# Row maxima of batch 0 and of half of batch 1 are placed inside the second pair's front, GpSimd rotates batch 3, and inputs are loaded and projected batch by batch

## The reference

```python
q = (jnp.einsum('bsd,ed->bse', x, Wq) + bq).reshape(b, s, H, HD).transpose(0, 2, 1, 3)
k = (jnp.einsum('bsd,ed->bse', x, Wk) + bk).reshape(b, s, KVH, HD).transpose(0, 2, 1, 3)
v = (jnp.einsum('bsd,ed->bse', x, Wv) + bv).reshape(b, s, KVH, HD).transpose(0, 2, 1, 3)
q = _rms_norm(q)
k = _rms_norm(k)
cos, sin = _rope_tables(s, q.dtype)
q = _apply_rope(q, cos, sin)
k = _apply_rope(k, cos, sin)
...
attn = jnp.einsum('bhqd,bhkd->bhqk', q * scale, k)
attn = jnp.where(causal[None, None], attn, -jnp.inf)
attn = jax.nn.softmax(attn, axis=-1)
out = jnp.einsum('bhqk,bhkd->bqhd', attn, v).reshape(b, s, d)
return jnp.einsum('bsd,ed->bse', out, Wo) + bo
```

## Time and profile before

| | |
|---|---|
| median of 3 runs | 509.94 us (508.55 to 512.79) |
| the profiled execution | 507.93 us, its span 506.2 us |
| PE, PEld busy | 402.6 us (80%), 312.7 us (62%) |
| DVE, ACT, POOL busy | 343.6 us (68%), 242.7 us (48%), 107.5 us (21%) |
| first weight transpose, first projection | 9.98 us, 14.46 us |
| first stack transpose, first row maximum on TensorE | 39.24 us, 64.74 us |
| first exp_scores of layer 0 | 78.99 us |

### The profile page before, as it was taken

How to read it: one execution, slowest core, us unless ns; L and a number is a source line. 1 busy time by engine, 2 the same in 40 slices (tenths; PEclk the granted TensorE clock), 3 DMA queues, 4 the chain that set the end, 5 groups by cost and what they waited for, 6 DMA issues and landing times.

```text
span 506.2 us, 8074 instructions
## 1 busy us (share of the span) xinstructions
PE 402.6 (80%) x3090; PEld 312.7 (62%) x3090; DVE 343.6 (68%) x782; ACT 242.7 (48%) x432; POOL 107.5 (21%) x111
## 2 busy tenths in 40 slices
PE   2906578998885554599998688999987899999993
PEld 2506545676644443378766565667766689888883
DVE  0489698777677749576648888656946485666545
ACT  1558714655433863367557714446535324422230
POOL 4400005449311630042183000000101710000001
PEclk9957598999897886579999999999989999999998
DMA  6900020000000000000000006970000000000101
GB/s 203 296 5 1 1 70 5 3 4 1 2 2 0 0 2 0 0 1 0 3 0 1 1 1 87 116 149 3 2 0 1 0 2 1 0 1 0 43 1 42
DMA packets 13126, 13.33 MB, mean 26 GB/s; under 512 B 2904, under 2 KB 12448, under 8 KB 12832
## 3 DMA queue, kind: packets, MB, share of 16 engines
q1 hardware_dynamic: 12224, 12.54, 11.3%
q10 hardware_dynamic: 864, 0.27, 0.3%
HBM read 11.56 MB, written 1.05 MB: 25 GB/s over the span
## 4 chain that ended last, share of the span: by engine, by line
PE 60%; DVE 21%; ACT 11%; issue 3%; POOL 1%; DMA 1%; SPq 0%; DVEq 0%; POOLq 0%; ACTq 0%
PE PS L2146 12%; PE PS L2163 6%; ACT arena L750 5%; PE PS L1761 4%; PE PS L1845 4%; DVE mx L1263 3%; PE PS L2073 3%; PE PS L383 3%; PE PS L1886 3%; PE PS L2086 3%; PE PS L1813 3%; PE PS L1739 2%; PE PS L1855 2%; PE PS L1642 2%; DVE arena L1152 2%
## 5 line engine op out<-in xcount | busy, mean ns | idle before, releaser
L869 ACT ACTIVATE PT<-PS 128x512 f32<-128x512 f32 x96 | 53.5, 594 | 36.3 <-PE PS L1813 36.2
L2146 PE MATMUL PS<-arena_r 128*128 128x512 f32 x264 | 64.6, 393 | 2.2 <-ACT xT L750 2.2
L666 POOL TENSOR_SCALAR va<-mv 128x4 f32<-128x4 f32 x12 | 5.3, 443 | 273.3 <-DVE mv L1099 273.3
L2146 PEld LDWEIGHTS PS<-arena_r 128*128 128x128 f32 x264 | 48.0, 188 | 11.9 <-issue 2.7
L750 ACT ACTIVATE arena<-PS 96x1024 bf16<-96x1024 bf16 (+4 forms) x59 | 44.5, 810 | 22.5 <-PE PS L1739 11.3
L1739 PE MATMUL PS<-ident,arena 128*96 128x128 bf16 x416 | 30.7, 241 | 28.9 <-DVE arena L1142 27.5
L1739 PEld LDWEIGHTS PS<-ident,arena 128*96 128x96 bf16 x416 | 28.7, 141 | 32.7 <-DVE arena L1142 29.2
L1761 PE MATMUL PS<-masks,ident 128*128 128x512 bf16 x112 | 43.2, 386 | 4.7 <-DVE mx L1263 2.4
L1263 DVE TENSOR_REDUCE mx<-PS 128x4 f32<-128x1024 f32 x32 | 39.0, 1218 | 1.2 <-PE PS L1793 0.2
L2163 PEld LDWEIGHTS PS<-arena_r 128*128 128x128 f32 x264 | 34.4, 191 | 2.5 <-DVE arena_r L1564 0.9
L2163 PE MATMUL PS<-arena_r 128*128 128x256 f32 x264 | 35.1, 283 | 0.7 <-DVE arena_r L1564 0.7
(11 more groups left out here) (218 smaller groups left out, 904.7 us busy)
## 6 DMA issues: line engine op xcount, KB each, us to landing
arena<-in_L_ffn_w SPq DMA_DIRECT2D x16, 176.0 KB, 10.2
arena<-in_L_ffn_w SPq DMA_DIRECT2D x2, 1024.0 KB, 10.2
arena<-in_L_ffn_w SPq DMA_DIRECT2D x2, 704.0 KB, 7.5
arena<-in_fside_BxS2xS SPq DMA_DIRECT2D x1, 1024.0 KB, 12.7
out<-x SPq DMA_DIRECT2D x4, 256.0 KB, 2.5
x<-in_x SPq DMA_DIRECT2D x1, 768.0 KB, 8.6
arena<-in_L_attn_Wq SPq DMA_DIRECT2D x2, 256.0 KB, 4.5
arena<-in_L_attn_Wo SPq DMA_DIRECT2D x2, 256.0 KB, 6.4
```

The costliest lines, as they stand in the source:

```text
L869: nc.scalar.activation(PT[:, n % 2, 512 * j:512 * (j + 1)], bank(3 + j), ACT.Exp, scale=NEG_SCALE)\
L2146: last = mm(bank(2 * (n % 2) + gu), wp[c][:, gu, c_ * P:(c_ + 1) * P], xp[5][:, c, blk * 512:(blk + 1) * 512], start=(step == 0 and c == 0 ...
```

## The change

- **Loads.** SP issues ident, Wq, then x in three transfers (batch 0; batch 1; batches 2 and 3), each with a semaphore of its own for what waits; Wk and Wv go to the head of ScalarE's queue. The count of semaphores is kept down by dropping unused ones.
- **Projection batch by batch.** TensorE transposes batch 0, projects tiles 0 and 1, transposes batches 1 and 2, projects tiles 2 and 3, transposes batch 3 and projects the rest. ScalarE's copy of batch 3 goes behind its first squares. The waits for tables and constants stand after the projections.
- **GpSimd rotates batch 3** with seven instructions of its own; it starts when VectorE has normed the second pair (`qk_normed`), and hi_part(3) waits for `last_rotated`.
- **Maxima early.** EARLY is 6: the four groups of batch 0 and two of batch 1 stand in the front. VectorE takes two groups after the thresholds, one after each rem_part of the second pair, splits batch 0's maxima, and takes the other two between its stack copies. All six use banks 0 to 2. On TensorE batch 0's four groups stand ahead of the stack transposes of batch 2, and batch 1's two behind those of batch 2 and of batch 3.
- **ScalarE's order.** abs_sums moves from ahead of hi_part(0) to behind the stack copies of batch 0, and writes to another place; hi_part(2) goes ahead of batch 1's stack copies, hi_part(3) behind them and woT's copy.

The diff, cut:

```diff
-        def score_set(m):
-
+        EARLY = NG + 2
+
+        def score_set(L, m):
+
+            if L == 0 and m < EARLY:
+                return 0
             return 3 * (1 - m % 2) if m < LAG * NG else 0
...
             sp.dma_start(ident[:, :], t["ident"]).then_inc(w["ident"], 16)
+            sp.dma_start(wq0n[:, 0:2, :], t["L0_attn_Wq"].rearrange("(r p) d -> p r d", p=P)).then_inc(w["l0"], 16)
             sp.dma_start(x[:, 0:2, :], xv[:, 0:2, :]).then_inc(x_loaded, 16)
-            sp.dma_start(wq0n[:, 0:2, :], t["L0_attn_Wq"].rearrange("(r p) d -> p r d", p=P)).then_inc(w["l0"], 16)
-            sp.dma_start(wq0n[0:64, 2, :], t["L0_attn_Wk"]).then_inc(w["l0"], 16)
-            sp.dma_start(wq0n[64:128, 2, :], t["L0_attn_Wv"]).then_inc(w["l0"], 16)
-            sp.dma_start(x[:, 2:TT, :], xv[:, 2:TT, :]).then_inc(x_rest_loaded, 16)
+            sp.dma_start(x[:, 2:4, :], xv[:, 2:4, :]).then_inc(x1_loaded, 16)
+            sp.dma_start(x[:, 4:TT, :], xv[:, 4:TT, :]).then_inc(x_rest_loaded, 16)
...
+            def rotate(b):
+
+                pool.wait_ge(qk_normed, b // 2 + 1)
+                pool.wait_ge(w["const"], LOADS["const"])
+                pool.wait_ge(A[0]["lo"], b - 1)
+                hf = HD // 2
+                for k in range(2):
...
+                    pool.tensor_tensor(ri, qi, cos, ALU.mult)
+                    pool.tensor_tensor(si[:, :, 0:hf], qi[:, :, hf:HD], s1, ALU.mult)
+                    ins = pool.tensor_tensor(si[:, :, hf:HD], qi[:, :, 0:hf], s2, ALU.mult)
+                alone(ins)
+                ro, sq = (z[:, b % 2].rearrange("p t n -> p (t n)") for z in (qro, qsq))
+                alone(pool.tensor_tensor(ro, ro, sq, ALU.add), last_rotated)
+
+            rotate(B - 1)
...
             w = w_loaded
+            act.dma_start(wq0n[0:64, 2, :], t["L0_attn_Wk"]).then_inc(w["l0"], 16)
+            act.dma_start(wq0n[64:128, 2, :], t["L0_attn_Wv"]).then_inc(w["l0"], 16)
...
+                    evac_xT(0, 3, 4)
+
+                    hi_part(L, 0)
+                    hi_part(L, 1)
+                    mid_part(L, 0)
+                    mid_part(L, 1)
+                    squares(2)
+                    squares(3)
+                    evac_stacks(L, 0)
                     abs_sums()
...
+                    hi_part(L, 2)
+                    evac_stacks(L, 1)
+                    evac_groups(act, copy, NG0 - 1, NG0, "act")
+                    hi_part(L, 3)
+                    mid_part(L, 2)
+                    mid_part(L, 3)
+                    evac_stacks(L, 2)
+                    evac_stacks(L, 3)
                     return
...
+                    normed_queries_and_keys(2)
+                    rotate(2)
+                    thresholds()
+                    row_maxima(0, 0, 0, 0, None)
+                    row_maxima(0, 0, 1, 1, None)
+                    rem_part(0, 2)
+                    row_maxima(0, 0, 2, 2, None)
+                    rem_part(0, 3)
+                    row_maxima(0, 0, 3, 3, None)
+                    split_maxima(0, 0)
+                    lo_part(0, 2)
+                    lo_part(0, 3)
+                    evac_stacks(0, 2)
+                    row_maxima(0, 1, 0, NG, None)
+                    evac_stacks(0, 3)
+                    row_maxima(0, 1, 1, NG + 1, None)
...
                 if L == 0:
-                    for tt in range(TT):
+                    transpose_x(0, 0, 1)
+                    copied_out(pe, NG0 - 1)
+                    project_tile(0)
+                    project_tile(1)
+                    transpose_x(0, 1, 3)
+                    project_tile(2)
+                    project_tile(3)
+                    transpose_x(0, 3, 4)
+                    for tt in range(4, TT):
                         project_tile(tt)
...
                 def max_scores(b, g, m, between):
-                    set_ = score_set(m)
-                    if m >= 2 * NG:
+                    set_ = score_set(L, m)
+                    in_turn = m >= 2 * NG or (L == 0 and 1 <= m < EARLY)
+                    if in_turn:
 
                         pe.wait_ge(a["mx"], 2 * m - 1)
...
+                if L == 0:
+                    pe.wait_ge(a["ev_act"], TG[0])
+                    for g in range(NG):
+                        max_scores(0, g, g, None)
+                    stack_transposes(0, 2)
+                    pe.wait_ge(a["ev_act"], 2 * TG[0])
+                    max_scores(1, 0, NG, None)
+                    stack_transposes(0, 3)
+                    max_scores(1, 1, NG + 1, None)
```

More of the change, by code:

```diff
@@ L1223, in attn_front @@
                     read_projections(1)
[L1224 to L1238 removed]
+                    normed_queries_and_keys(0)
+                    rotate(0)
+                    rotate(1)
+                    rem_part(0, 0)
+                    rem_part(0, 1)
+                    read_projections(2)
+                    read_projections(3)
+                    lo_part(0, 0)
+                    lo_part(0, 1)
+                    normed_queries_and_keys(2)
[14 more added lines that the diff above has]
+                    row_maxima(0, 1, 1, NG + 1, None)
                 else:
@@ L1748, in attn_back @@
                 causal = L == 0
-                last_n = B * TG[L] - 1
-                for n in range(last_n - 3, last_n + 1):
-                    who, count = stack_evac(L, n)
-                    pe.wait_ge(a["ev_" + who], count)
-                pe.wait_ge(krow_set, L + 1)
                 def kv(h):
@@ L1888, in project_outputs @@
                     last.then_inc(y_ready, 1)
+                if L == 0:
[7 more added lines that the diff above has]
+                    max_scores(1, 1, NG + 1, None)
+                last_n = B * TG[L] - 1
+                for n in range(last_n - 3, last_n + 1):
+                    who, count = stack_evac(L, n)
+                    pe.wait_ge(a["ev_" + who], count)
+                pe.wait_ge(krow_set, L + 1)
                 for step in range(STEPS):
@@ L1899, in attn_back @@
                             values(n - 1)
-                        if step < B:
+                        if step < B and (L == 1 or step * NG + g >= EARLY):
                             max_scores(step, g, step * NG + g, n - 1 if n >= 1 else None)
```

97 lines of the change are left out of this document (41 added, 56 removed).

## The result

The changed kernel takes 516.73 us (median of 4, 515.7 to 519.17), the kernel before 509.49 (median of 4): ratio 1.013, 95% interval 1.008 to 1.018. The forecast was 519.0 in a range of 512.0 to 524.6. The profiled run took 515.70 us with a span of 513.9, against 507.93 and 506.2 before: 7.8 us more where 9.1 were forecast. The first exponent scores of batch 0, to which the prediction follows the change, start at 86.07 instead of 78.99, 7.08 later.

The account below looks back on a forecast made before the run. The prediction followed the chain through layer 0's front to batch 0's first exponent scores: 91.5 against 79.0, +12.5, less 0.4 given back and 3.0 for the start, +9.1, so 519.0 us. Range 515 to 523, ends 512.3 and 524.6.

Parts of the forecast that it names:

- Start: First loads and projections: TensorE starts near 5.9 instead of 9.98; gain taken as 3.0 us, from 2.1 to 4.1.
- the prediction's own lower case: Start of TensorE: at its lower clock level tiles 0 and 1 take until 13.9, leaving a gain of 2.1 us.
- GpSimd's rotation: Batch 3's rotation on GpSimd alternates with VectorE's: rotate(2) ends at 53.3 instead of 49.1; lower bound costs 1.2, not 3.8.
- What is queued behind: ScalarE after rotate(2): hi_part(2) until 55.4, five copies until 60.0, woT until 60.7, when TensorE's first row maximum starts.
- Maxima: Six early groups on one bank set, 2.3 us each, ahead of stack transposes: the last of these ends at 82.6, against 63.8.
- SP's queue: Batch 0's rows of maxima wait behind late loads (5.6 us), then take 3.1: scores at 91.5.
- Give-back: After batch 0's scores: batch 1's split is ready where TensorE waited about 1.9 us; 0.4 us taken, 0 to 1.9.
- GpSimd barely delays VectorE: Rival on the rotation: 2.6 to 4.2 us less than forecast, 515 to 516.4 us; chance 0.17.
- the idle time is really filled: Rival: early maxima use VectorE's idle time in the front; 503.7 us with the start; chance 0.07.
- SP's loads are not in the way: Rival: mT rows go out between the loads, or issues shrink without the one stall: 514 to 517 us; chance 0.08.
- The low clock stays: Rival: TensorE's low clock lasts over all early maxima and batch 3's transposes: +4.7, 523.7 us; chance 0.12.

Follow-up runs that it names:

- a_rows_first: The changed kernel with SP issuing batch 0's three transfers of maxima ahead of the eight late loads: 512.0 us, ratio 1.005 to the kernel before.
- a_both: The changed kernel with rotate(3) back on VectorE and batch 0's three transfers of maxima ahead of the late loads: 512.3 us, ratio 1.006 to the kernel before.
- b_start: The kernel before with only the new order of first loads and projections batch by batch: 508.1 us, ratio 0.996.
- a_rot_dve: The changed kernel with rotate(3) back on VectorE, behind rotate(2): 516.6 us, ratio 1.014 to the kernel before.
- b_one_early: The kernel before with the new start, thresholds early and one group of row maxima brought into the front's gaps: 506.1 us, ratio 0.994.

## Why the prediction was right

The sign, the size and the mechanism held: the moved maxima stand in front of the front's own steps, the last stack transpose moves from 63.75 to 78.84, and the rows of maxima then wait behind the late loads. Point by point, in the changed kernel's own time (the forecast's less 3.0):

- *Start.* Forecast 3.0 earlier at qss, measured 1.8, and 0.74 at rotate(2). The step that was mis-sized twice: tiles 0 and 1 were given 1.3 us each and took 2.5 each, which is the prediction's own lower case (13.9 for their end, measured 14.0, though that case is reckoned with the low clock and the granted clock reads 1.00); and GpSimd's bias additions, in no term of it, met the norm's operations and took 1.1. (Its own sum is off by 0.2 as well: 19.81 less 15.5 is 4.3, not 4.1. The 3.0 is chosen and doesn't hang on it.)
- *GpSimd's rotation.* Forecast 4.2 us on rotate(2) (seven operations 6.9), lower bound 1.2, measured 2.5 (5.2), the same in four kernels. "They alternated" was right, but they overlap in part: 4.6 us of GpSimd's six products cost 2.5.
- *What is queued behind.* hi_part(2) ended at 52.97 (52.4 forecast), the five copies at 57.5 (57.0), first maximum on TensorE at 58.05 (57.7). ScalarE's order was read rightly.
- *Maxima.* Pitch 2.15 and 2.67 with rem_part between (2.3 and 2.7 forecast). Last stack transpose 78.84 (79.6).
- *SP's queue.* The late loads came first, as forecast, but took 4.05 us and not 5.62: the 2.18 us of one issue in the kernel before is no fixed part of it (0.48 to 2.75 over the runs). Rows to landing 3.1, as forecast. Exp scores at 86.07, forecast 88.5.
- *Give-back.* Forecast 0.4 us back, measured 0.6 more lost by the end of the span (7.08 at the exp scores, 7.7 there). Batch 1's split was ready, but the 3.44 us of idle time sent TensorE to its low clock for the second group of scores; a_rows_first shows that this alone was 1.8.

So the total is better than its parts, and that is luck: errors of 1 to 2.4 us on both sides cancel. At rotate(2)'s end the start's missing 2.3 and the rotation's 1.7 too many nearly cancel (50.86 against 50.3); from there the walk to the last stack transpose was 1.3 too long and the issues 1.6, and the give-back 1.0 too good: 9.1 - 2.4 + 1.0 = 7.7. The rivals: *GpSimd barely delays VectorE* would have had 1.2 where 2.5 was measured, and *the idle time is really filled* falls by the first maximum, at 58 and not before 53. *SP's loads are not in the way* falls by a_rows_first: the rows did wait, and going first was worth 4.7 us. Half of its condition came true, though: the issues shrank without the one stall among them, by 1.6 us. *The low clock stays* holds in part: 0.52 from 53.9 to 61.5 and 0.50 from 86.0 to 90.5, but 1.00 from 61.5 to 67.5. The 0.52 from 70.8 to 75, under the transposes of batch 2, the forecast had itself.

The Trainium skill ("SBUF — State Buffer", Who interferes with whom) says that a VectorE tensor_tensor with both inputs in SBUF contends with GpSimd's reads, that tensor_scalar can too, in its two-port modes, and that tensor_reduce never does. All three agree with rows here: products 0.32 to 0.98, the two TENSOR_SCALARs 0.20 to 0.77, reductions 1.49 and 1.22 unchanged beside GpSimd. That the other engine "fully blocks" for a whole instruction is not borne out at 2.5 us lost beside 4.6. The second of the three points to the collision at 21 us, if the two operations there run in such a mode, which no run shows.

## What to carry to other kernels

Before work is moved forward into idle time, look at which steps the idle engine is waiting for, and put the moved work behind nothing that leads to them: six groups of maxima ahead of rem_part, lo_part and the stack transposes cost, with ScalarE's order, some 5 us (a_both at 1.006 against b_start at 0.996), while one or two groups in the gaps brought some 2 or 3 (506.1 and 505.1 against 508.1). When a step moves, follow the queue entries that it releases: here loads that before had been over 4.7 us ahead of three small transfers now stood right in front of them, when everything waited for the three. One line of order in SP's block was worth 4.7 us. And a step that goes from one engine to another only helps if the two don't slow each other down: here 2.6 us taken off VectorE stretched what it did at that time by 2.5. Check also what an earlier start now meets.

## What the runs showed of the hardware

- An idle time of TensorE can cost more than its length: 3.44 us of it were followed by 4.5 us at 0.50 (3.42 us in a_rot_dve too), 1.18 us in a_rows_first by 4.5 us at 1.00. But length alone doesn't decide. The same 1.9 us of idle time near 129 us was followed by 0.68 or 0.73 in two kernels and by 1.00 in two others, and in the kernel before none of the idle times between 64.7 and 75 us was over 1.33, yet 75 to 77 ran at 0.55. What decides there is open; near 129 it took the 1.7 us that separated these kernels in the front.
- At its start TensorE worked at half pace: in the changed kernel eight projecting matmuls took 5.00 us from 9.00 on, eight 2.85 from 15.13 on; in b_one_early 5.20 from 10.30 on and 2.85 from 16.62 on. The kernel before, whose TensorE began 5 us later, at 9.98, was at full pace from 14.46 on: 32 projecting matmuls in 10.49. The granted clock reads 1.00 for all of it (the first of the three columns at a row's end, here of the changed kernel), so it doesn't show the cause.

```profile
9.00:14.00 5.00, 5.00 (x10) 2.80 (x11) 0.62 (x2) 0.00 (x0) 0.00 (x0) 1.00 0.95 235
```
- The same kernel's span went from 505.9 to 512.9 us with its mean granted clock from 0.928 to 0.901. Differences under 2 us between two kernels can hardly be read from a median of ten.
- VectorE's TENSOR_SCALAR with one input in SBUF was stretched beside GpSimd by nearly as much (0.20 to 0.77) as a TENSOR_TENSOR with two (0.32 to 0.98).
